# Two-quad prelude, order of the expert work and norm from PSUM banks in a fused attention, Strassen MLP and expert kernel

## The reference

```
attn = softmax((x Wq)(x Wk)^T / sqrt(512)) (x Wv) Wp + bp
cms  = gelu(attn cW1 + cb1) cW2 + cb2 + one_hot(code)
mod  = gelu([attn, cms] mW1 + mb1) mW2 + mb2
x1   = clip(x + cms + mod, 0, 1)
h    = gelu(x1 W_down[e] + b_down[e]) W_up[e] + b_up[e] + x1      # e: one of 3 experts for each sequence
out  = layernorm(h) * ln_w[e] + ln_b[e]
```

## Time and profile before

| | us |
|---|---|
| median of 3 runs | 1131.21 |
| the profiled execution's own time | 1133.84 |
| its span | 1132.1 |
| TensorE busy | 1064.7 (94%) |
| VectorE busy | 810.8 (72%) |
| ScalarE busy | 501.3 (44%) |
| GpSimd busy | 6.5 (1%) |

### The profile page before, as it was taken

The page is one execution under the profiler, slowest core; times in us unless marked ns, Lnnn a source line. Parts: engine busy times, 40 slices in busy tenths (PEclk is TensorE's granted clock), DMA queues, the critical chain, the costliest instruction groups (busy, mean ns, idle before and its releaser), DMA issues. The chain is left out here.

```text
span 1132.1 us, 13953 instructions
## 1 busy us (share of the span) xinstructions
PE 1064.7 (94%) x4985; PEld 884.5 (78%) x4985; DVE 810.8 (72%) x1413; ACT 501.3 (44%) x881; POOL 6.5 (1%) x11
## 2 busy tenths in 40 slices
PE   8999799999999899999999959999999989999975
PEld 6788588888877688888798848888887768888764
DVE  4434886776678887877555988677667888787767
ACT  4425645444254444334354545454425544433350
POOL 0000000000000000000000000000000000000001
PEclk9999899999999999999999969999999999999988
DMA  6500221120243232305507032312023323231341
GB/s 224 186 1 12 64 75 38 41 71 19 75 141 101 92 132 75 130 20 202 195 28 167 23 130 75 112 39 73 19 76 138 104 88 136 75 131 56 98 126 75
DMA packets 55518, 103.69 MB, mean 92 GB/s; under 512 B 3166, under 2 KB 31898, under 8 KB 51354
## 3 DMA queue, kind: packets, MB, share of 16 engines
q1 hardware_dynamic: 55360, 102.78, 27.1%
q10 hardware_dynamic: 90, 0.02, 0.0%
HBM read 81.82 MB, written 20.97 MB: 91 GB/s over the span
## 5 line engine op out<-in xcount | busy, mean ns | idle before, releaser
L1005 DVE TENSOR_TENSOR acc<-bank,acc 128x512 f32<-128x512 f32 x224 | 154.0, 688 | 85.3 <-PE bank L216 85.1
L631 ACT ACTIVATE sbc<-sbc,bias 128x512 f32<-128x512 f32 x112 | 81.0, 724 | 282.8 <-DVE sbc L975 218.5
L214 PE MATMUL bank<-hid_hi,w_lo 128*128 128x512 f32 x512 | 200.7, 392 | 4.4 <-DVE hid_lo L901 1.7
L214 PE MATMUL bank<-ta_hi,w_lo 128*128 128x512 f32 x448 | 179.6, 401 | 26.3 <-DVE sbc L975 16.5
L215 PE MATMUL bank<-hid_hi,w_hi 128*128 128x512 f32 x512 | 199.7, 390 | 0.0
L216 PE MATMUL bank<-hid_lo,w_hi 128*128 128x512 f32 x512 | 199.6, 390 | 0.0
L216 PE MATMUL bank<-ta_lo,w_hi 128*128 128x512 f32 x448 | 177.7, 397 | 0.0
L215 PE MATMUL bank<-ta_hi,w_hi 128*128 128x512 f32 x448 | 177.5, 396 | 0.0
L214 PEld LDWEIGHTS bank<-ta_hi,w_lo 128*128 128x128 f32 x448 | 86.2, 192 | 50.9 <-DVE sbc L975 18.9
L975 DVE TENSOR_TENSOR sbc<-bank,sbc 128x512 f32<-128x512 f32 x144 | 97.5, 685 | 36.3 <-PE bank L216 34.7
L214 PEld LDWEIGHTS bank<-hid_hi,w_lo 128*128 128x128 f32 x512 | 96.3, 188 | 28.2 <-issue 3.4
(11 more groups left out here) (208 smaller groups left out, 1562.2 us busy)
## 6 DMA issues: line engine op xcount, KB each, us to landing
...
```

The lines of the kernel that those rows point to most:

```text
L214: nc.tensor.matmul(dst, w_l, a_h, start=start, stop=False, **kw)
L631: nc.scalar.activation(dst, dst, ACT.Gelu, **kw).then_inc(g_done[key], 1)
L1005: nc.vector.tensor_tensor(dst, bank[:, :], dst, ALU.add).then_inc(evac, 1)
```

## The change

- b_up is loaded as columns (eight small DMAs, one transpose, one copy) and added to x1 in `acc` by eight ScalarE activations a pair (`act_up_bias`), after `xp` is made and before `pe_up` reads it. `dve_z` and `dve_stats` are gone. `dve_norm` reads the banks, in two halves of two tiles, each with a power of its own on GpSimd.
- Attention of batch 1: y(2), down(0), transposes, y(3), up(0), scores(2), down(1), values(2), scores(3), up(1), values(3), attends. The ScalarE, VectorE and SP programs follow; the norms stand ahead of each softmax's or value tile's work. Banks are given out anew.
- In all batches the probabilities are transposed before the last value tile, and `act_x` writes all x_hi first and the float copies later.
- The prelude runs both quads woven into one another, 14 groups ahead of the loop; quad 1 has a sum buffer `s_g` of its own, and the order of token blocks changes.
- Turn: x_lo in two halves, the clips of the first pair after the evacuation with k = 6.
- Tail: three staging buffers; pieces 4 and 5 are loaded at it = 22 and converted at it = 25, pieces 0 and 1 at it = 24 after the third evacuation, pieces 2 and 3 in a buffer of their own. The TensorE order of the tail stays.

The diff, cut to its core:

```diff
-    ln_v = (b_up, ln_w, ln_b)
+    ln_v = (ln_w, ln_b)
+    bup_v = b_up.rearrange("e (k p) -> (e k) p", p=P)
...
+        s_g = at("s_g", X0 + 52 * KB, [P, 4, 2, P])
...
-        ao = at("ao", SB0 + 8 * KB, [P, 2, KT, TB])
+        ao = at("ao", ACC0, [P, 2, KT, TB])
...
+        e_raw = [at(f"e_raw{k}", o, [P, 2, EW]) for k, o in enumerate((W1R, W2R, X0 + 48 * KB))]
...
-        T_ORDER = ("B11", "B21", "T1", "T2", "T3", "B22", "T4")
+        T_ORDER = ("B11", "B21", "T1", "B22", "T2", "T3", "T4")
...
+        TR_BANK, Y_BANK, S_BANK, V_BANK = (0, 0, 0, 4), (4, 4, 4, 0), (0, 0, 0, 4), (4, 4, 0, 4)
+        E_STAGE = ((0, 0, 0, 0, 0, 0, 0, 0), (0, 0, 1, 1, 2, 2, 0, 0))
+        E_LANDS = ((1, 1, 2, 2, 3, 3, 4, 4), (5, 5, 1, 1, 1, 1, 6, 6))
+        E_RANK = ((0, 1, 2, 3, 4, 5, 6, 7), (0, 1, 4, 5, 2, 3, 6, 7))
...
+                if i and t == TT - 1:
+                    pe_probs_T(pe, n - 1)
+                    pe_probs_T(pe, n)
...
+            if b:
+                pe_down(pe, n - 2)
             pe_tr(pe, n + 1)
             pe_y(pe, n + 1)
-            pe_scores(pe, n)
-            pe_values(pe, n)
-            if b:
-                pe_down(pe, n - 2)
-            pe_scores(pe, n + 1)
-            pe_values(pe, n + 1)
             if b:
                 pe_up(pe, n - 2)
+            pe_scores(pe, n)
+            if b:
                 pe_down(pe, n - 1)
-            pe_probs_T(pe, n)
-            pe_probs_T(pe, n + 1)
-            pe_attend(pe, n)
+            pe_values(pe, n)
+            pe_scores(pe, n + 1)
             if b:
                 pe_up(pe, n - 1)
+            pe_values(pe, n + 1)
...
+            for i, which in ((0, 1), (0, 2), (1, 1), (1, 2), (0, 5), (1, 5), (0, 3), (0, 6), (1, 6), (1, 3), (0, 7), (1, 7),
+                             (0, 4), (1, 4)):
+                (first if which in (1, 2, 5, 6) else second)(i, which)
...
+                new, old, dn = it < QB, 2 <= it - 1 < QB, has_l2(it - 2)
...
-            for k in (3, 0, 1, 2) if n and n % 2 == 0 else range(KT):
+            order = (3, 0, 1, 2) if n == 2 else range(KT)
+            for k in order:
                 act.wait_ge(tr_mm[k], n + 1)
-                if n and n % 2 == 0 and k == 3:
-                    act.wait_ge(l2_mm, 8 * (RB * (n // 2) - 1))
-                act_copy((xs if n >= 2 else xf)[:, n % 2, k, :], ps[k][:, :])
-                act_copy(x_hi[:, n % 2, k, :], ps[k][:, :]).then_inc(x_h[k], 1)
-
-        def act_tiles(act, landed, n0, bank0, dst, done):
-            for k in range(4):
+                if n == 2 and k == 3:
+                    act.wait_ge(l2_mm, 8 * (RB - 1))
+                act_copy(x_hi[:, n % 2, k, :], ps[TR_BANK[n] + k][:, :]).then_inc(x_h[k], 1)
...
+        def act_up_bias(act, n):
+            bb, pp = divmod(n, 2)
+            for j in range(KT):
+                act.wait_ge(xp_l, 4 * n + j + 1)
+                for s in range(SEQ):
+                    c0 = (2 * n + s) * KT + j
+                    part = acc[:, j, pp * TB + s * T:pp * TB + (s + 1) * T]
+                    last = nc.scalar.activation(part, part, ACT.Identity, bias=bu_all[:, c0:c0 + 1])
+                last.then_inc(xb_done, 1)
...
-            cms_t = {10: ("B11", "B21"), 11: ("T1",), 12: ("T2", "T3"), 13: ("B22",), 14: ("T4",)}
+            cms_t = {10: ("B11", "B21"), 11: ("T1", "B22"), 12: ("T2", "T3"), 14: ("T4",)}
...
+                if not tail and it >= QB:
+                    for k in (0, 1) if it == QB else (4, 5):
+                        act_expert_piece(act, b, k)
...
             act_x(act, n)
             if b:
+                act_xp(act, n - 2)
                 act_expert_piece(act, b - 1, 0)
                 act_expert_piece(act, b - 1, 1)
-            act_tiles(act, y_mm, 4 * n, 4, lambda k: y_hi[0][:, k, :], y_h)
+                act_up_bias(act, n - 2)
+            act_y(act, n)
+            if b:
+                act_down(act, n - 2)
             act_x(act, n + 1)
             if b:
                 act_expert_piece(act, b - 1, 2)
                 act_expert_piece(act, b - 1, 3)
-            act_tiles(act, y_mm, 4 * n + 4, 4, lambda k: y_hi[1][:, k, :], y_h)
+            act_y(act, n + 1)
             if b:
-                act_xp(act, n - 2)
-            act_exps(act, n)
-            act_tiles(act, v_mm, 4 * n, V_BANK[n], lambda k: vv_hi[0][:, k, :], v_h)
-            if b:
-                act_down(act, n - 2)
+                act_xp(act, n - 1)
                 act_expert_piece(act, b - 1, 4)
                 act_expert_piece(act, b - 1, 5)
+                act_up_bias(act, n - 1)
+            act_exps(act, n)
+            if b:
+                act_down(act, n - 1)
+            v_tiles(0, range(TT))
+            if b:
+                act_expert_piece(act, b - 1, 6)
+                act_expert_piece(act, b - 1, 7)
             act_exps(act, n + 1)
             if b:
                 act.wait_ge(xd_out, 32 * b)
-            act_tiles(act, v_mm, 4 * n + 4, V_BANK[n + 1], lambda k: vv_hi[1][:, k, :], v_h)
-            nc.scalar.activation(warm[:, :], bias[:, 0:1], ACT.Gelu)
-            if b:
-                act_xp(act, n - 1)
-                act_expert_piece(act, b - 1, 6)
-                act_expert_piece(act, b - 1, 7)
-                act_down(act, n - 1)
+            v_tiles(1, range(TT - 1))
             act_probs_T(act, n)
             act_probs_T(act, n + 1)
+            v_tiles(1, (TT - 1,))
+            nc.scalar.activation(warm[:, :], bias[:, 0:1], ACT.Gelu)
             act_ao(act, n)
             act_w1_first(act, b, 0, 0)
             act_w1_first(act, b, 0, 1)
             act_w1_second(act, b, 0)
             act_t(act, b, 0, "B11")
             act_t(act, b, 0, "B21")
+            act_w1_first(act, b, 1, 0)
             act_ao(act, n + 1)
-            act_w1_first(act, b, 1, 0)
+            act_w1_first(act, b, 1, 1)
             act_t(act, b, 0, "T1")
-            act_w1_first(act, b, 1, 1)
+            act_s(act, b, 0, 1)
+            act_t(act, b, 0, "B22")
             act_t(act, b, 0, "T2")
+            act_w1_second(act, b, 1)
+            act_s(act, b, 0, 5)
+            act_s(act, b, 1, 1)
             act_t(act, b, 0, "T3")
-            act_t(act, b, 0, "B22")
+            act_s(act, b, 1, 5)
+            act_s(act, b, 0, 2)
             act_t(act, b, 0, "T4")
+            act_s(act, b, 1, 2)
 
         def act_expert_last(act):
             bb = NBAT - 1
...
+        def dve_norm(dve, n):
             bb, pp = divmod(n, 2)
+            bank0 = 0 if pp else 4
+            dve.wait_ge(ln_in[pp], 64 * (bb + 1))
+            for h in range(2):
+                tiles = (2 * h, 2 * h + 1)
+                for t in tiles:
+                    dve.wait_ge(up_mm, 4 * n + t + 1)
+                    nc.vector.bn_stats(stat[:, t, :], ps[bank0 + t][:, :]).then_inc(st_done, 1)
+                for t in tiles:
+                    dve.wait_ge(st_done, 4 * n + t + 1)
+                    nc.vector.bn_aggr(mv[:, t, :], stat[:, t, :]).then_inc(ag_done, 1)
+                dve.wait_ge(ag_done, 4 * n + 2 * h + 2)
+                nc.vector.tensor_scalar_add(veps[:, 2 * h:2 * h + 2],
+                                            mv[:, 2 * h:2 * h + 2, 1:2].rearrange("p t o -> p (t o)"), LN_EPS)\
+                    .then_inc(ve_done, 1)
+                for t in tiles:
+                    nc.vector.scalar_tensor_tensor(out=z_tile(pp, t), in0=ps[bank0 + t][:, :], scalar=mv[:, t, 0:1],
+                                                   in1=ln_p[n][:, t // TS, 0, :], op0=ALU.subtract, op1=ALU.mult)\
+                        .then_inc(z_cent, 1)
+                dve.wait_ge(rstd_done, 2 * n + h + 1)
+                for t in tiles:
+                    dve.wait_ge(z_cent, 4 * n + t + 1)
+                    nc.vector.scalar_tensor_tensor(out=z_tile(pp, t), in0=z_tile(pp, t), scalar=rstd[:, t:t + 1],
+                                                   in1=ln_p[n][:, t // TS, 1, :], op0=ALU.mult, op1=ALU.add)\
+                        .then_inc(z_done[pp], 1)
+            nc.vector.tensor_copy(bu_all[:, :], ps[4][:, 128:128 + B * KT]).then_inc(bias_ready, 1)
...
+            v_tiles = lambda i, tiles: dve_tiles(dve, v_h, 4 * (n + i), V_BANK[n + i], lambda k: vv_hi[i][:, k, :],
+                                                 lambda k: vv_lo[i][:, k, :], v_l, tiles)
             if b == 0:
                 dve_x_lo(dve, n)
             else:
+                dve_xp(dve, n - 2)
                 dve_expert_piece(dve, b - 1, 0)
                 dve_expert_piece(dve, b - 1, 1)
-            dve_tiles(dve, y_h, 4 * n, 4, lambda k: y_hi[0][:, k, :], lambda k: y_lo[0][:, k, :], y_l)
+            dve_y(dve, n)
+            if b:
+                dve_h3(dve, n - 2)
             dve_x_lo(dve, n + 1)
             if b == 0:
                 dve_columns(dve)
             else:
                 dve_expert_piece(dve, b - 1, 2)
                 dve_expert_piece(dve, b - 1, 3)
```

(81 more changed lines are left out.)

417 lines of the change are left out of this document (176 added, 241 removed).

## The result

The changed kernel takes **1092.07 us** (median of 4 runs, 1091.72 to 1092.37); the kernel before, run beside it, takes 1131.62 us. The ratio is 0.9648, its 95% interval 0.9636 to 0.966, so 39.5 us are gone. The profiled execution took 1092.1 us, its span is 1090.3.

What follows compares the result with a forecast made beforehand. TensorE, busy 94% of the span, was taken as the bound, losing time in waits: 7.6 + 13.4 + 3.6 + 0.95 + 0.8 - 1.0 + 12.3 - 3.4 = 34.3 us off 1133.84, less a 2.6 offset: 1097 us, range 1091 to 1103.

Steps and rivals of the forecast that it cites:

- rival (b): Whole kernel: the weave works better than, no stretch at 0.50, no loss in the middle; 1092 us, chance 0.11.
- Preludes: Both MLP preludes: woven groups and norms moved out leave 5.2 us lost instead of 12.8 and 18.6; gain 7.6 + 13.4.
- Under 0.5 us before group 5: Prelude, sign of being right: TensorE's wait before group 5 of quad 0 is under 0.5 us.
- 15 groups ahead of the first layer-2 product: Prelude, sign of being right: batch 0's first layer-2 matmul about 30 us after the first attend ends, 15 groups behind it.
- End of attention: Batch 0: transposing probabilities before the last value tile covers their copies and subtractions, and a 0.50 stretch goes; gain 1.9 + 1.7.
- x first: Batch 0: ScalarE writes x_hi before the float copies, so the first x_lo is 0.5 us sooner in both tiles; gain 0.95.
- Second attention: Batch 1: down and up products move ahead; waits of 1.5 and 0.8 us go, one of 1.3 is new; gain 0.8.
- rival (c): Second attention: norms ahead of the softmax run 2 to 8 us late, so TensorE waits; 1106 to 1115 us, chance 0.09.
- Turn: Before y of batch 1: one 2.7 us wait replaces three short ones, as clips precede the last evacuation; gain 0.
- Middle: Middle of the MLP: B22 of the second region moves into an iteration with more VectorE work; 0.5 us per batch, loss 1.0.
- Tail: Kernel's end: pieces 4 and 5 loaded early remove the 7.69 us wait, and norms shorten to 8.8 to 9.1; gain 12.3.
- Clock: TensorE's granted clock: seven new waits bring two stretches at 0.50; loss 3.4, bounds 0 to 8.5.

Runs made afterwards that it cites:

- experiments 4 and 5: Changed kernel with the old prelude order on all three engines: 1111.68 us; that kernel plus 13 unread VectorE statistics in the second prelude: 1117.67 us.
- the copy's run: Changed kernel with each bank copied to SBUF ahead of the statistics in all four norms: 1097.39 us, 5.3 more than the changed kernel.

## Why the prediction was right, and where it was not

The forecast was 1097 us, the measurement 1092.07, inside the range and on the value of rival (b): no loss in the middle, and nearly no clock loss.

**Preludes** (7.6 + 13.4 forecast). By the windows 12.8 and 18.6 us of loss became 3.8 and 3.9, a gain of 9.0 and 14.7. The stages hold 8.1 and 14.1, with the middle and, in each, the stretch at 0.50 that came or went there. Near in size and right in both reasons, as experiments 4 and 5 show: 6.0 us for the norm where the forecast had 5.8 (13.4 - 7.6). The single waits were less well placed: T1 lo costs 0.99 us of idleness where 0.3 was walked, and c22, hid_lo and the next iteration cost less than walked. By the walk 5.2 us would be lost in each. "Under 0.5 us before group 5" was wrong, "15 groups ahead of the first layer-2 product" came true.

**End of attention** (1.9 + 1.7). The size is right: with the x copies the forecast has 4.55 us up to the first MLP matmul, and the table has 2.9 + 1.6. The reason was right and incomplete. The last value tile does cover the copies and subtractions, with 2.4 us to spare. But the copies were late because of a table load of 1.28 us ahead of them, whose move stood in the diff and was not costed, and which removes all but 0.3 us of the wait without the transposes' new place. That the size came right is no evidence for the one cause that the prediction named.

**x first** (0.95): 0.9 us at the first two places, 0.4 more in batch 1.

**Second attention** (0.8): 0.9. The walk's details hold, too: one wait of 1.33 us for x_lo behind four gelus, none after it, and rival (c) had nothing behind it, since even 2.5 us more in each norm (the copy's run) made no wait there.

**Turn** (0; one wait of 2.7 us instead of three): one of 2.19 us idle, released by the last evacuation, which stands behind the clips as the forecast had it. With the clips behind it, 1.3 us less.

**Middle** (-1.0). The term should have been nothing. The idle times around it are the same as in the kernel before; the iteration that took B22 had room. That is 1.0 us that the forecast had too little.

**Tail** (12.3): 10.3 + 4.2 - 0.5 = 14.0 us. Idle times of 1.05 and 0.34 us before the last evacuations where 0.6, 1.2 and 0.8 were walked; no wait between down(2) and down(3), and 17.2 us of norms behind h3 lo, as said. A norm takes 8.6 us, not 9.1, which is 1 us in two; statistics from a bank cost no more than from SBUF, as the forecast had taken it. The eight activations of the up bias took 3.3 us and not 2.9. The experiments give the shares: 8.5 us for the staging buffers with the early conversion, 5.3 for the pass over the banks.

**Clock** (-3.4): the term that was most mis-sized. I gave the new waits two stretches at 0.50 beyond those that stayed. One is new, at 376 us, and one is gone behind the same wait of batch 1, where TensorE had 0.50 at 927 us before; so the term came out as nothing. In all, one stretch is left where before had seven. Whether one and the same wait draws a stretch differs from kernel to kernel, as the last section tells, so this term can only be given as bounds.

In all, the two traces differ by 41.8 us where the sum had 34.3. Of these 7.5 us the clock term is 3.4, preludes and middle together 2.2, the tail 1.7 and the rest 0.2. The prediction had taken off 2.6 us, since the profiled execution of before was that much above its median; this leaves the 4.9 us between forecast and measurement. Most errors of size point the same way: what was walked came out dearer than it was.

The parts undone one at a time sum to 19.6 + 6.0 + 5.2 + 2.0 + 8.5 + 5.3 = 46.6 us, 7 more than the whole. That remainder was not taken apart. The clock may hold some of it: the trace with the old prelude alone has 20.4 us at 0.50 ahead of TensorE's end, that of the changed kernel 3.4.
